# A Mamba block with feed-forward on one core: the drawn instruction lists replaced, last out products moved behind the last sums, two more buffers for copied transposes

## The reference

```
xi, z = split(x @ W_in.T)                       # 2 x 512 channels
u = silu(conv4(xi) + conv_b)                    # causal, 4 taps, per channel
dbl = u @ W_xproj.T                             # 16 for dt, 16 B, 16 C
dt = softplus(dbl[:16] @ W_dt.T + b_dt)
h = h * exp(dt * -exp(A_log)) + dt * u * B      # per channel and state, over tokens
y = (sum over states of h * C + u * D_skip) * silu(z)
x1 = layernorm(x + y @ W_out.T)
out = layernorm(x1 + (silu(x1 @ wg.T) * (x1 @ wu.T)) @ wd.T)    # hidden 768
```

## Time and profile before

| | us |
|---|---|
| median of 3 runs | 1764.86 (1763.44 to 1766.13) |
| the profiled execution, its own time | 1763.22 |
| its span in the trace | 1761.2 |
| first scan, last scan's end | 29.36, 1701.56 |
| busy: PE, PEld | 1706.4, 1226.4 |
| busy: DVE, ACT, POOL | 1580.5, 1589.5, 1502.0 |

### The profile page before, as it was taken

The page is one execution under the profiler, slowest core; times in us unless marked ns, Lnnn a source line. Parts: engine busy times, 40 slices in busy tenths (PEclk is TensorE's granted clock), DMA queues, the critical chain, the costliest instruction groups (busy, mean ns, idle before and its releaser), DMA issues.

```text
span 1761.2 us, 40344 instructions
## 1 busy us (share of the span) xinstructions
PE 1706.4 (97%) x15806; PEld 1226.4 (70%) x15806; DVE 1580.5 (90%) x1817; ACT 1589.5 (90%) x2736; POOL 1502.0 (85%) x913
## 2 busy tenths in 40 slices
...
GB/s 216 1 123 1 45 79 4 133 1 101 36 4 132 3 133 2 51 85 4 133 1 100 36 28 108 4 133 1 63 74 4 132 1 135 1 28 97 25 13 13
DMA packets 172144, 100.59 MB, mean 57 GB/s; under 512 B 139538, under 2 KB 158738, under 8 KB 163892
## 3 DMA queue, kind: packets, MB, share of 16 engines
...
## 4 chain that ended last, share of the span: by engine, by line
PE 65%; ACT 21%; issue 6%; DVE 5%; SPq 1%; DMA 1%; POOL 0%; ACTq 0%; DVEq 0%; POOLq 0%
PE tp L1178 19%; PE ring L1199 16%; PE yb L1192 9%; PE ring L1297 9%; ACT hT L786 6%; PE ring L1273 6%; DVE h L966 4%; ACT decay L779 4%; ACT L779 1%; ACT u L807 1%; ACT res L838 1%; PE ring L1255 1%; ACT sz L812 1%; PE ring L1264 1%; ACT L812 1%
## 5 line engine op out<-in xcount | busy, mean ns | idle before, releaser
L633 POOL TENSOR_TENSOR drive<-dtu,b_all 128x1024 f32<-128x1024 f32 x511 | 1198.2, 2383 | 16.8 <-DVE h L966 15.5
L779 ACT ACTIVATE decay<-dt,a_neg 128x512 f32<-128x512 f32 x1024 | 689.5, 703 | 28.7 <-DVE h L966 24.9
L966 DVE TENSOR_TENSOR_SCAN h<-decay,h,drive 128x512 f32<-128x512 f32 x512 | 620.1, 1270 | 46.1 <-ACT decay L779 45.6
L966 DVE TENSOR_TENSOR_SCAN h<-decay,drive 128x512 f32<-128x512 f32 x512 | 590.2, 1210 | 63.1 <-ACT decay L779 56.9
L786 ACT ACTIVATE hT<-tp 128x512 f32<-128x512 f32 x1024 | 570.9, 602 | 78.2 <-PE tp L1178 73.9
L1178 PEld LDWEIGHTS tp<-ident,h 128*128 128x128 f32 x4096 | 464.6, 142 | 213.2 <-issue 100.9
L1178 PE MATMUL tp<-ident,h 128*128 128x128 f32 x4096 | 562.0, 278 | 27.8 <-ACT hT L786 25.1
L1192 PE MATMUL yb<-hT,diag_c 128*32 128x128 f32 x8192 | 260.1, 276 | 0.0
L1199 PE MATMUL ring<-xt,w_in 128*128 128x512 f32 x512 | 242.3, 603 | 5.1 <-ACT xi L797 2.6
L1192 PEld LDWEIGHTS yb<-hT,diag_c 128*32 128x32 f32 x8192 | 214.9, 110 | 41.8 <-issue 36.2
L1199 PE MATMUL ring<-xt,w_u 128*128 128x512 f32 x360 | 169.9, 598 | 1.7 <-DVE hid L1013 1.7
...
## 6 DMA issues: line engine op xcount, KB each, us to landing
...
c_col<-bc_scratch SPq DMA_DIRECT2D x256, 2.0 KB, 2.5
...
```

The costliest lines, as they stand in the source:

```text
L633: tt(drive[:, j % 4, :, :], src, b_all[:, n:n + 2, :], ALU.mult).then_inc(g_dr, 1)
L779: act(decay[decay_slot(k.parity, i)][:, :], dt[:, k.parity, cb, :], ACT.Exp, scale=a_neg[:, cb, n:n + 1]).then_inc(a_da, 1)
L966: nc.vector.tensor_tensor_scan(h[:, h_slot(k.parity, q), at:at + T, i % 4], decay[decay_slot(k.parity, i)][:, :], drive[:, (i // 2) % 4, i ...
```

## The change

No arithmetic changes. There are four edits.

1. `HTS` goes from 10 to 12: twelve buffers for copied transpositions.
2. `dt` of channel blocks 0 and 1 has one buffer for both parities; blocks 2 and 3 keep two. This is the room for the two `hT` buffers. The wait of `softplus` on `g_dtu` follows.
3. PE_END is written anew: the out products of blocks 0 to 2 stand later in it.
4. All tables (FIRST, ODD, EVEN, LAST of PE, ACT, DVE and POOL, and the SP lists) are drawn anew.

```diff
-HTS = 10
+HTS = 12
...
-    (14, 0): [("sum", 11)], (14, 3): [("sum", 12), ("turn", 2)], (15, 3): [("dt", 1), ("sum", 13)],
+    (13, 1): [("turn", 1), ("turn", 2)], (14, 3): [("sum", 12), ("dt", 0)], (15, 0): [("dt", 1)],
+    (15, 2): [("sum", 13)],
...
-    (15, 3): [("hT", 59), ("sp", 1)],
+    (14, 1): [("hT", 54), ("hT", 55), ("sp", 0), ("sp", 1)], (14, 2): [("hT", 56)],
...
-    (0, 1): [("xi", 0)], (0, 3): [("sum", 14), ("sum", 15)], (1, 0): [("turn", 3)], (1, 1): [("xi", 1)],
+    (0, 1): [("sum", 14)], (0, 3): [("xi", 0), ("sum", 15)], (1, 1): [("turn", 3), ("xi", 1)],
...
-    (0, 0): [("hT", 60), ("hT", 61)], (0, 2): [("hT", 62), ("hT", 63)], (1, 0): [("y", 3), ("xi", 0)],
+    (0, 1): [("hT", 60), ("hT", 61)], (0, 2): [("hT", 62)], (0, 3): [("hT", 63)],
+    (1, 0): [("xi", 0), ("y", 3)], (1, 1): [("hT", 0), ("hT", 1)], (2, 0): [("hT", 2), ("hT", 3), ("xi", 1)],
...
-    (15, 3): [("r2", 1), ("t2", 0), ("t2", 1), ("skip", 2), ("m2", 0), ("m2", 1)],
+    (15, 2): [("r2", 1), ("t2", 1), ("m2", 1), ("skip", 1), ("skip", 2)],
...
-    ("end_out", 0, 0), ("end_out", 0, 1), ("end_out", 0, 2), ("end_out", 1, 0), ("end_T", 60), ("end_T", 61), ("end_out", 1, 1), ("end_T", 62), ("end_T", 63),
-    ("end_sum", 14), ("end_sum", 15), ("end_out", 1, 2), ("end_turn",), ("end_out", 0, 3), ("end_out", 1, 3),
+    ("end_T", 60), ("end_T", 61), ("end_sum", 14), ("end_T", 62), ("end_T", 63), ("end_out", 0, 0), ("end_out", 0, 1),
+    ("end_sum", 15), ("end_out", 0, 2), ("end_turn",), ("end_out", 1, 0), ("end_out", 1, 1), ("end_out", 0, 3),
+    ("end_out", 1, 2), ("end_out", 1, 3),
...
-        dt = sb("dt", [P, 2, CB, T])
+        dt = sb("dt", [P, CB + 2, T])
...
+        def dt_block(k, cb):
+
+            return cb if cb < 2 or k.parity == 0 else cb + 2
...
-                wait(eng, g_dtu, k.count(2, p - 3))
+                wait(eng, g_dtu, k.count(2, -1 if p == 0 else -2))
+                at = dt_block(k, 2 * p)
```

More of the change, by code:

```diff
@@ L51 @@
 PE_FIRST = {
[L52 to L56, removed]
-    (14, 0): [("sum", 11)], (14, 3): [("sum", 12), ("turn", 2)], (15, 3): [("dt", 1), ("sum", 13)],
+    (0, 1): [("xi", 0), ("z", 0)], (0, 3): [("xi", 1), ("xi", 2)], (2, 2): [("xi", 3)],
@@ new lines @@
+    (1, 3): [("xi", 2)], (2, 1): [("out", 0, 0), ("out", 0, 1)], (2, 3): [("out", 1, 0)], (3, 1): [("xi", 3)],
+    (3, 3): [("out", 1, 1)], (4, 1): [("sum", 0), ("sum", 1)], (4, 3): [("z", 0), ("z", 1)],
+    (5, 1): [("sum", 2), ("sum", 3)], (5, 2): [("z", 2)], (5, 3): [("z", 3)],
+    (6, 1): [("x1T", 0), ("x1T", 1)], (6, 3): [("turn", 0), ("gate", 0), ("gate", 1), ("sum", 4), ("sum", 5)],
+    (7, 1): [("gate", 2)], (7, 3): [("up", 0)], (8, 1): [("xproj", 0)],
+    (8, 3): [("dt", 0), ("sum", 6), ("sum", 7)], (9, 1): [("gate", 3), ("up", 1)], (9, 3): [("up", 2)],
@@ L97 @@
+    (10, 1): [("up", 3)], (10, 3): [("dt", 1), ("sum", 8), ("sum", 9)], (11, 1): [("gate", 4), ("gate", 5)],
+    (11, 2): [("up", 4)], (12, 0): [("up", 5)], (12, 1): [("turn", 1)], (12, 3): [("sum", 10), ("sum", 11)],
+    (13, 1): [("down", 0, 0), ("turn", 2)], (13, 3): [("down", 0, 1)], (14, 1): [("sum", 12)],
     (14, 3): [("down", 1, 0)], (15, 1): [("down", 1, 1)], (15, 3): [("sum", 13)],
@@ L134 @@
 PE_LAST = {
[L135 to L140, removed]
@@ L141 @@
-    (8, 3): [("gate", 5)], (9, 1): [("up", 2)], (9, 3): [("sum", 6), ("sum", 7)], (10, 1): [("up", 3)],
-    (10, 3): [("up", 4)], (11, 1): [("up", 5)], (11, 3): [("sum", 8), ("sum", 9)], (12, 0): [("turn", 1)],
-    (12, 2): [("down", 0, 0)], (13, 0): [("down", 0, 1)], (13, 2): [("sum", 10)], (14, 0): [("sum", 11)],
-    (14, 2): [("down", 1, 0)], (15, 0): [("down", 1, 1)], (15, 1): [("turn", 2)],
-    (15, 3): [("sum", 12), ("sum", 13)],
+    (0, 3): [("sum", 14), ("sum", 15)], (1, 2): [("turn", 3)], (1, 3): [("z", 0)], (2, 0): [("z", 1)],
@@ new lines @@
+    (2, 1): [("out", 0, 0), ("out", 0, 1)], (3, 0): [("out", 1, 0)], (3, 2): [("sum", 0)],
+    (4, 0): [("out", 1, 1)], (4, 2): [("z", 2)], (4, 3): [("z", 3), ("sum", 1), ("sum", 2)],
+    (5, 0): [("sum", 3)], (5, 1): [("x1T", 0), ("x1T", 1)], (5, 3): [("gate", 0)], (6, 1): [("up", 0)],
+    (6, 3): [("gate", 1), ("turn", 0)], (7, 0): [("sum", 4)], (7, 2): [("gate", 2)], (7, 3): [("gate", 3)],
+    (8, 1): [("gate", 4)], (8, 3): [("gate", 5)], (9, 1): [("sum", 5), ("sum", 6), ("sum", 7)],
+    (9, 3): [("up", 1)], (10, 1): [("up", 2)], (10, 3): [("up", 3)], (11, 1): [("up", 4), ("up", 5)],
@@ L146 @@
+    (11, 3): [("sum", 8), ("sum", 9)], (12, 1): [("down", 0, 0)], (12, 3): [("down", 0, 1)],
+    (13, 1): [("down", 1, 0)], (13, 3): [("sum", 10), ("sum", 11)], (14, 0): [("down", 1, 1)],
+    (14, 2): [("turn", 1)], (14, 3): [("turn", 2)], (15, 1): [("sum", 12)], (15, 3): [("sum", 13)],
 }
@@ L177 @@
 PE_EVEN = {
-    (0, 1): [("xi", 0)], (0, 3): [("sum", 14), ("sum", 15)], (1, 1): [("turn", 3), ("xi", 1)],
-    (1, 3): [("out", 0, 0), ("out", 0, 1)], (2, 1): [("xi", 2)], (2, 3): [("out", 1, 0)],
-    (3, 1): [("sum", 0), ("sum", 1)], (3, 3): [("out", 1, 1)], (4, 1): [("xi", 3)], (4, 3): [("z", 0)],
-    (5, 1): [("z", 1)], (5, 2): [("sum", 2), ("sum", 3), ("z", 2), ("z", 3)],
-    (6, 0): [("x1T", 0), ("x1T", 1), ("sum", 4), ("turn", 0), ("gate", 0), ("gate", 1)], (6, 2): [("up", 0)],
-    (7, 0): [("gate", 2)], (7, 2): [("sum", 5)], (8, 0): [("xproj", 0)], (9, 0): [("dt", 0)],
@@ L184 @@
-    (9, 1): [("sum", 6), ("sum", 7)], (9, 3): [("up", 1), ("up", 2)], (10, 1): [("gate", 3)],
+    (0, 1): [("xi", 0)], (0, 3): [("sum", 14), ("sum", 15)], (1, 1): [("turn", 3)], (1, 2): [("xi", 1)],
+    (1, 3): [("out", 0, 0)], (2, 1): [("out", 0, 1)], (2, 3): [("xi", 2)], (3, 0): [("out", 1, 0)],
+    (3, 2): [("sum", 0), ("sum", 1)], (4, 0): [("out", 1, 1)], (4, 2): [("xi", 3)], (5, 0): [("z", 0)],
+    (5, 2): [("z", 1), ("sum", 2), ("sum", 3)], (5, 3): [("z", 2), ("z", 3)],
+    (6, 0): [("x1T", 0), ("x1T", 1)], (6, 2): [("turn", 0), ("gate", 0), ("gate", 1), ("sum", 4)],
@@ L185 @@
+    (7, 0): [("up", 0)], (7, 1): [("sum", 5)], (7, 3): [("gate", 2)], (8, 3): [("xproj", 0)],
+    (9, 1): [("dt", 0), ("sum", 6), ("sum", 7)], (9, 3): [("up", 1), ("up", 2)], (10, 1): [("gate", 3)],
     (10, 3): [("up", 3)], (11, 1): [("dt", 1), ("sum", 8), ("sum", 9)], (11, 3): [("gate", 4), ("up", 4)],
-    (12, 1): [("gate", 5)], (12, 3): [("up", 5), ("sum", 10), ("sum", 11)],
-    (13, 1): [("down", 0, 0), ("down", 0, 1)], (13, 2): [("turn", 1)], (14, 0): [("sum", 12)],
-    (14, 1): [("turn", 2)], (14, 3): [("down", 1, 0)], (15, 1): [("down", 1, 1)], (15, 3): [("sum", 13)],
+    (12, 1): [("gate", 5)], (12, 3): [("up", 5), ("sum", 10), ("sum", 11)], (13, 0): [("turn", 1)],
@@ L216 @@
+    (10, 1): [("hid", 2)], (10, 3): [("gs", 3), ("hid", 3)], (11, 3): [("gs", 4)], (12, 0): [("hid", 4)],
+    (12, 2): [("gs", 5)], (13, 0): [("hid", 5)], (13, 2): [("skip", 1)], (14, 1): [("skip", 2)],
+    (14, 3): [("r2", 0)], (15, 3): [("t2", 0), ("r2", 1), ("m2", 0), ("t2", 1), ("m2", 1)],
 }
 POOL_EVEN = {
-    (2, 0): [("diag", 1), ("diag", 2), ("diag", 3), ("gate", 3)],
-    (6, 1): [("std", 0), ("heads", 0), ("dtu", 1)],
-    (11, 1): [("dtu", 0), ("gate", 0), ("std", 1), ("norm", 1)],
@@ L221 @@
-    (15, 1): [("diag", 0), ("gate", 1), ("gate", 2)],
+    (2, 0): [("diag", 1), ("diag", 2), ("diag", 3), ("gate", 3)], (6, 1): [("std", 0), ("heads", 0)],
+    (7, 0): [("dtu", 1)], (9, 1): [("std", 1)], (10, 1): [("norm", 1)], (12, 1): [("gate", 0)],
+    (13, 1): [("dtu", 0)], (15, 1): [("gate", 1), ("diag", 0), ("gate", 2)],
 }
-SP_EVEN = [("spread", 0), ("bload", 0), ("bload", 1), ("bload", 2), ("bload", 3), ("xt", 0), ("store", 0), ("res", 0)]
+SP_EVEN = [("spread", 0), ("xt", 0), ("bload", 0), ("bload", 1), ("bload", 2), ("store", 0), ("bload", 3), ("res", 0)]
@@ L665, in dt_times_u @@
                 wait(eng, g_dr, k.count(32, -32 + 16 * (half + 1)))
-                tt(dtu[:, two, :], dt[:, k.parity, two, :], u[:, k.parity, two, :], ALU.mult).then_inc(g_dtu, 1)
+                at = dt_block(k, 2 * half)
+                tt(dtu[:, two, :], dt[:, at:at + 2, :], u[:, k.parity, two, :], ALU.mult).then_inc(g_dtu, 1)
             def scale_and_shift(k, norm):
@@ L778, in decay_step @@
                     wait(eng, a_dt, k.count(4, 2 * (i // 32) + 2))
-                act(decay[decay_slot(k.parity, i)][:, :], dt[:, k.parity, cb, :], ACT.Exp,
+                act(decay[decay_slot(k.parity, i)][:, :], dt[:, dt_block(k, cb), :], ACT.Exp,
                     scale=a_neg[:, cb, n:n + 1]).then_inc(a_da, 1)
```

61 lines of the change are left out of this document (31 added, 30 removed), and 124 rows, old and new, of tables (ACT_EVEN, ACT_FIRST, ACT_LAST, ACT_ODD).

## The result

The changed kernel takes 1767.25 us (median of 22 runs, 1766.09 to 1768.29) against 1764.41 for before (22 runs, 1762.96 to 1767.47). The ratio is 1.0015, 95% interval 1.0009 to 1.0021. That is 2.8 us slower, within the 0.2% that I took for no change, where 1757.8 and "faster" had been forecast. The profiled execution takes 1768.27 us, its span 1766.3, 5.1 us over that of before.

What follows compares the result with a forecast made beforehand. PE was taken as the bound from chunk 1 to 15, with ACT fullest in chunk 0. Terms -2.2 - 2.5 - 2.7 + 0 + 0.3 = -7.1 us gave a median of 1757.8; 8-in-10 range 1750.5 to 1766.

Steps and rivals of the forecast that it cites:

- Chunks 0 and 1: First two chunks: joining both softplus pairs in chunk 0 saves two table loads; -2.5 us, bounds -5 and +2.
- chunk 1 by -3.2: Chunk 1: loses its 3.2 us excess over later odd chunks once the late softplus leaves the end of chunk 0.
- The block's +1.1: Softplus block at (14, 1) of chunk 0: two more activations lengthen it by 1.1 us, DVE standing about 4.2.
- Odd chunks: Six odd chunks: block 3's turn no longer waits for ACT's copy of the last sum; 0.45 us each, -2.7.
- Even chunks: Seven even chunks: transposition runs still wait for copies; no change taken, bounds -0.5 and +1.5 us each.
- third rival: Even chunks: transpositions 57 to 61 wait for copies behind late decays; 1.8 to 2.25 us each, 1770 to 1774, chance 0.13.
- first rival: Whole kernel: new lists also close PE's remaining idle time; 1748 to 1754 us, middle 1751.5, chance 0.17.
- Chunk 15: Last chunk: one more group of sums is drawn, +0.3 us; its 2.0 idle may move by 1.5 either way.
- The end: After the last scan: reordered out products fill PE's waits; -2.2 us, bounds 2.5 gain and nothing.
- The 0.3 for sums that stand apart: End: PE's changes between separated sums and other matmuls cost 0.3 us, bounds 0 and 0.6.
- Buffers and DMA places: Whole kernel: twelve `hT` buffers, the single dt buffer and moved DMAs among SP's waits cost nothing.

Runs made afterwards that it cites:

- e1: The changed kernel with chunk 0's `heads` entry in POOL's list moved back from (12, 0) to (8, 0): 1758.82 us.
- e2: The kernel before with only chunk 0's `heads` entry moved from (8, 0) to (12, 0) in POOL's list: 1770.17 us.
- e13: The changed kernel with chunk 0's `heads` entry at (8, 1), one drive behind its place in before: 1761.04 us.
- e7: e1 with the copy of transposed block 57 in odd chunks moved from (15, 3) to (15, 2) in ACT's list: 1751.57 us.
- e8: e1 with the five lists of the last chunk taken from before, the new end kept: 1756.49 us.
- e10: e7 with the last chunk's lists taken from before: 1750.09 us.
- e11: e10 with the copy of block 30 in even chunks at (8, 1) instead of (8, 2): 1748.97 us.
- e3: The changed kernel with all five lists of chunk 0 taken from before: 1764.52 us.
- e9: The kernel before with block 3's turn in odd chunks moved from (1, 0) to (1, 1) in PE's list: 1764.7 us.
- e12: The kernel before with the copy of block 57 in odd chunks moved from (15, 0) to (15, 3): 1772.37 us.
- e4: The kernel before with only the new PE_END order: 1762.47 us.
- e5: The kernel before with only the buffers changed (twelve `hT`, one dt buffer for the first pair), all lists kept: 1765.15 us.

## Why the prediction was wrong

**Chunks 0 and 1** (-2.5) is the step that failed: the two chunks together are 3.7 us longer (214.1 against 210.4). It costed ACT's items there one by one and disposed of the rest with "since DVE and POOL have their own lists in chunk 0". POOL's list held the dearest edit: `heads` from (8, 0) to (12, 0), a term put at nothing without a reason. The runs show that it costs 8.0 to 8.4 us on the median by e1, 6.2 by e2, and 1.8 to 2.2 for one drive by e13. With the entry back, the two chunks take 208.0 in e1 and 205.6 to 206.3 in e7, e8, e10 and e11, so 2.5 to 4.9 less than before (in e7, e10 and e11 a few tenths of it are copy 57's, which stands in chunk 1 too). So the forecast of -2.5 held, or was too small, for all that it had looked at. What to read was in before's trace: POOL's 15 waits at its `heads` row, one convolution of 1250 ns that overlaps a drive, and eleven of 740 that do not. The pieces that were priced: chunk 1 by -3.2 (measured -3.23, and e3 ties it to chunk 0's lists). The block's +1.1 was too small by DVE's wait, 6.0 instead of 4.2, but chunk 0 as a whole gave that back.

**Odd chunks** (-0.45 each): +0.15 came out. The mechanism came true as far as it goes: in after the turn waits no longer, and nothing waits behind it, at the start of odd chunk 7:

```profile
778.19 0.63 PE L1267 MATMUL ring<-ident,yg 128*128 128x128 f32 x4
778.65 1.88 PE L1202 MATMUL ring<-xt,w_in 128*128 128x512 f32 x4
```

But in the same chunk a new wait for a copy, put at nothing, took more away (next point). What the turn's own wait was worth stays open: in before's lists its removal gave nothing, as the wait went to the next product (e9); in the new lists it was not tried by itself.

**Even chunks** (0) and the third rival: even ones are 0.30 shorter, a pair 0.13. The rival's mechanism is there, copies behind the last decays, but it shows at the end of odd chunks. It costs 0.97 us a pair, not 1.8 to 2.25 a chunk; e7 takes it out for 7 us, and e12 puts it into before for 8. So the new lists win about 1.1 us a pair without it, and e7's 1751.57 is near the first rival's middle, 1751.5. That the forecast would have been nearly met without the move of `heads` is luck: 7 us lost to this copy and 2 in chunk 15, neither of them in the sum, stand against gains in the middle chunks that were forecast too small.

**Chunk 15** (+0.3): mis-sized. After takes 109.03 to the first addition and e4, with before's lists and the same end, 107.01: +2.0. With before's lists in e8 1.4 come back, as much as two of PE's waits grew by there (0.7 for the norm, 0.65 for `xi`). That these waits are the cause was not tried, and the other 0.6 is not accounted for.

**The end** (-2.2): right, -2.36 in e4. The 0.3 for sums that stand apart had no row behind it. In after two groups of 32 matmuls take 2.0 us (starts at 770.36 and 771.38 for one of them), where 64 together take 1.88 in the earlier trace rows, so 0.15 is nearer. In the change the gain of the end is cancelled by chunk 15 (-0.3 together).

**Buffers and DMA places** (0): e5 bears out the buffers in the lists of before. The DMA places were never tried apart.

**The sum** of measured terms: +8.5 - 3.2 - 1.2 - 0.3 + 1.3 = +5.1 in the profiled execution. Of it 1.6 ahead of the first scan and the 1.3 at the end lie in stretches that vary from run to run; the median says +2.8.
